# Expert results added into the output in memory, in place of a gather and an add at the end

## The chip, the cores and the metric

The kernel runs on one core of a Trainium2 chip. The metric is the device time of one execution in microseconds (us), taken as the median of three runs. The profile is of one further execution.

## The reference

The input has 4 sequences of 1024 tokens of 128 numbers, 4096 tokens in all. All is float32.

```python
x = x + attention(layernorm(x))        # scores (x*w_lhs)(x*w_rhs)^T, softmax, times layernorm(x)
x = x + experts(layernorm(x))
# experts, N = 4096 tokens, E = 8, hidden 512, TOP_K = 2:
probs = softmax(xf @ router_w.T); topk_probs, topk_idx = top_k(probs, 2)
topk_probs = topk_probs / sum(topk_probs)
h   = gelu(einsum('nc,ech->neh', xf, w_fc) + b_fc)
out = einsum('neh,ehc->nec', h, w_proj) + b_proj
y   = sum over a token's two experts of topk_prob * out
```

So each token has a value x after attention (called `res` here), and two expert results, each times its gate, are added to it.

## The kernel before, in words

Each engine has one instruction stream, written out by hand, and semaphores order them. The kernel has two stages.

**Attention** goes over four batches b (one sequence each, eight groups of 128 tokens). VectorE (DVE) adds the attention to the tokens in SBUF, in `res` (L1302), and raises `res_made` once for each half batch. Then the router picks two experts per token, and GpSimd (POOL) scatters each group of 128 tokens, twice, into the DRAM tensor `slots`, sorted by expert (`dispatch`, L721, 64 scatters). A row of `slots` carries the token's numbers, a row number made from the iota `row_id`, and its gate.

**Experts** go over NTILES = 40 tiles of W = 256 rows of one expert each, with buffers for NB = 8 tiles. The function `run_tiles` gives every engine the same walk: tiles 0 to 15 unrolled, the rest in a loop of eight and an unrolled end. Tiles 0 to 15 use tokens of the first three batches; the sixteen scatters of the last batch are done by POOL in steps 4 to 11 of this walk, two a step, and from tile 16 on SyncE (SP) loads only once all of them have landed (`all_dispatched`, L602 to L605).

For tile k:
- SP loads 256 rows of `slots` into `slots_in` (`load`, L613). From tile 8 on it first waits until DVE has taken the row numbers of an earlier tile.
- TensorE (PE) transposes two tiles ahead (L1146), computes the hidden layer (L1158 to L1160, semaphore `stepped`), and the output projection two tiles behind (L1175). ScalarE (ACT) splits and applies GELU (L911, L919).
- DVE copies gate and row numbers out of `slots_in` (`keep_rows`, L1548, L1549), adds the bias three tiles behind (L1556) and multiplies by the gate (`gate`, L1563, into one of eight buffers `gated`). Both wait on `returned[a]` until the scatters of the tile eight before, which used the same buffer, have landed.
- POOL gives tile k-4 back in step k (`give_back`, L787 to L791): it waits for `stepped`, `row_made` and `gated_made`, and issues two indirect DMAs of 128 rows of 512 bytes (H = 2) to the DRAM tensor `results`. Scatter after scatter goes out; POOL waits for no landing.

`wait_apart` (L505, L506) is a wait followed by a semaphore increment of its own instruction. Rows of a tile that carry no token go to spare rows of `results`, beyond the 8192 that are read.

**The end**: SP waits until all scatters have landed (L618), loads `results` into SBUF in four transfers of 1 MB (L622), DVE adds the two results of each token to `res` (L1592, L1594), and SP stores four parts of 512 KB to the output (L625) and waits for them.

Of the kernel before, what the change touches and what calls it, by code (L numbers as in the profile page):

```python
# [7 lines left out]
P = 128  # L8
F32 = mybir.dt.float32
# [4 lines left out]
ALU = mybir.AluOpType  # L14
# [7 lines left out]
def preln_attention_moe(nc, x, w_lhs, w_rhs, router_wT, w_fc, b_fc, w_proj, b_proj, out):  # L22
# [7 lines left out]
    NT = x.shape[1]  # L30
    D = x.shape[2]
# [3 lines left out]
    B = 4  # L35
    BT = NT // B
    S = BT * P
    N = NT * P
    K = 2
# [5 lines left out]
    H = 2  # L45
    W = H * P
    NB = 8
    NTILES = -(-((K * N + E * (W - 1)) // W) // NB) * NB
# [7 lines left out]


    SPARE = K * N + E * W
    results = nc.dram_tensor("results", [SPARE + NTILES * W, D], F32, kind="Internal").ap()
    assert D == P and NT % (B * 8) == 0 and E == 8  # L60

    with ExitStack() as ctx:  # L62
        def sb(name, shape, dt):
            return ctx.enter_context(nc.sbuf_tensor(name, shape, dt))

        def sem(name):
            return ctx.enter_context(nc.semaphore(name))
# [8 lines left out]
        res = sb("res", [P, NT, D], F32)  # L76
# [40 lines left out]
        raw_fc = sb("raw_fc", [P, E * HID], F32)  # L117
        raw_proj = sb("raw_proj", [P, E * HID], F32)
# [33 lines left out]
        row_id = sb("row_id", [P, NT, K], F32)  # L152
# [40 lines left out]
        gated = [[gated_all[:, a, h, :] for h in range(H)] for a in range(NB)]  # L193
        result_row = [sb(f"result_row{a}", [P, H], I32) for a in range(NB)]
# [49 lines left out]
        res_made = sem("res_made")  # L244
# [40 lines left out]
        gated_made = sem("gated_made")  # L285
        row_made = sem("row_made")
        returned = [sem(f"returned{a}") for a in range(NB)]
        results_in = [sem(f"results_in{b}") for b in range(B)]
        summed = sem("summed")
        added = sem("added")  # L290
        stored = sem("stored")

        block = ctx.enter_context(nc.Block())

# [207 lines left out]
        def wait_apart(eng, sem, value):  # L502


            eng.wait_ge(sem, value)  # L505
            eng.sem_inc(waited_apart, 1)  # L506

        def later(i, least=1):
            return not isinstance(i, int) or i >= least

        def run_tiles(eng, load_experts, step, lag, ahead, between):

            for first in range(0, EARLY, NB):
                load_experts(first)
                for a in range(NB):
                    step(first + a, a)
            between()  # L520
            last = NTILES // NB - ahead
            with eng.Fori(EARLY // NB, last) as i:
                load_experts(i * NB)
                for a in range(NB):
                    step(i * NB + a, a)
            for first in range(last * NB, NTILES, NB):
                load_experts(first)
                for a in range(NB):
                    step(first + a, a)
            load_experts(NTILES)  # L530
            for k in range(NTILES, NTILES + lag):
                step(k, k % NB)
# [37 lines left out]
        def turned_at(k):  # L570

            return k - 1 if not isinstance(k, int) else max(k - 1, 1)
# [6 lines left out]
        @block.sync  # L579
        def _(sp):  # L580
            sp.dma_start(res[:, 0:TU, :], x[:, 0:TU, :]).then_inc(x0_in, 16)
            sp.dma_start(res[:, TU:BT, :], x[:, TU:BT, :]).then_inc(x_in[0], 16)
            sp.dma_start(w_d[:, 0:1], w_lhs).then_inc(w_in, 16)
            sp.dma_start(w_d[:, 1:2], w_rhs).then_inc(w_in, 16)
            sp.dma_start(rwT[:, :], router_wT).then_inc(rw_in, 16)
            for b in range(1, B):
                sp.dma_start(res[:, b * BT:(b + 1) * BT, :], x[:, b * BT:(b + 1) * BT, :]).then_inc(x_in[b], 16)
            sp.dma_start(bfc[:, :, :], b_fc).then_inc(small_in, 16)
            sp.dma_start(bpr[:, :, :], b_proj.unsqueeze(0).to_broadcast([P, E, D])).then_inc(small_in, 16)
            sp.dma_start(raw_fc[:, :], w_fc.rearrange("c e h -> c (e h)")).then_inc(wfc_in, 16)  # L590
            sp.dma_start(raw_proj[:, :], w_proj.rearrange("p e c d -> p (e c d)")).then_inc(wpr_in, 16)

            sp.wait_ge(emptied, 32)
            sp.wait_ge(dispatched[0], 16 * K * 2 * BT)
            sp.wait_ge(dispatched[1], 16 * K * BT)
            sp.wait_ge(w_split, PIECES)
            sp.wait_ge(table_made, 1)

            def all_dispatched():
                for a in range(2):  # L600
                    sp.wait_ge(dispatched[a], 16 * K * 2 * BT)
                sp.wait_ge(table_made, 2)  # L602

            def load(k, a):
                start = sp.value_load(tile_start[0:1, bass.ds(k, 1)], min_val=0, max_val=E * N - W)  # L605

                if later(k, NB):


                    if isinstance(k, int) and k < NB + 3:  # L610
                        sp.wait_ge(stepped, turned_at(k - NB))
                    sp.wait_ge(row_made, k - NB + 2)
                sp.dma_start(xs[a], slots[bass.ds(start, W), :].rearrange("(p h) r -> p h r", h=H)).then_inc(xs_in[a], 16)  # L613
            run_tiles(sp, no_experts, load, 0, 0, all_dispatched)


            for a in range(NB):
                sp.wait_ge(returned[a], 16 * H * NTILES // NB)  # L618
            both = results[0:K * N, :].rearrange("(t p k) d -> p t (k d)", p=P, k=K)
            for b in range(B):  # L620
                half = (raw_fc, raw_proj)[b // 2][:, :].rearrange("p (t x) -> p t x", x=K * D)
                sp.dma_start(half[:, (b % 2) * BT:(b % 2 + 1) * BT, :], both[:, b * BT:(b + 1) * BT, :]).then_inc(results_in[b], 16)  # L622
            for b in range(B):
                sp.wait_ge(added, b + 1)
                sp.dma_start(out[:, b * BT:(b + 1) * BT, :], res[:, b * BT:(b + 1) * BT, :]).then_inc(stored, 16)  # L625
            sp.wait_ge(stored, 16 * B)

        @block.gpsimd
        def _(pool):
            for m in (ident, ident16):  # L630
# [5 lines left out]
                      allow_small_or_imprecise_dtypes=True).then_inc(consts, 1)  # L636
            pool.iota(next_slot[:, :], pattern=[[N, E]], base=0, channel_multiplier=0,
                      allow_small_or_imprecise_dtypes=True).then_inc(consts, 1)
            pool.iota(row_id[:, :, :], pattern=[[K * P, NT], [1, K]], base=0, channel_multiplier=K,
                      allow_small_or_imprecise_dtypes=True).then_inc(consts, 1)  # L640
            for of in (slice(0, EARLY), slice(EARLY, NTILES)):
                pool.iota(tile_id[:, of], pattern=[[1, of.stop - of.start]], base=0, channel_multiplier=0,
# [1 line left out]
            for a in range(NB):  # L644
# [14 lines left out]
                               base=0, pattern=[[1, P]], channel_multiplier=-1).then_inc(consts, 1)  # L659
            for m in (ident, ident16):  # L660
                pool.affine_select(out=m[:, :], in_=m[:, :], compare_op=ALU.not_equal, fill=1.0,
                                   base=0, pattern=[[-1, P]], channel_multiplier=1).then_inc(consts, 1)
# [122 lines left out]
            def give_back(k, a):  # L785

                pool.wait_ge(row_made, k + 1)  # L787
                wait_apart(pool, gated_made, k + 1)
                for h in range(H):
                    pool.indirect_dma_start(out=results[:, :], out_offset=bass.IndirectOffsetOnAxis(ap=result_row[a][:, h:h + 1], axis=0),  # L790
                                            in_=gated[a][h], in_offset=None).then_inc(returned[a], 16)  # L791


            def step(k, a):
                if later(k, 4):

                    pool.wait_ge(stepped, up_at(k) if tile_there(k) else min(k + 1, NTILES + 2))
                    give_back(k - 4, (a - 4) % NB)
                if isinstance(k, int) and 4 <= k < 4 + BT:
                    for i in range(K):  # L800
                        dispatch(B - 1, K * (k - 4) + i)
# [395 lines left out]
        def _(dve):  # L1197
# [386 lines left out]
            run_tiles(dve, expert_loader(dve, expert), step, 3, 0, lambda: dve.wait_ge(table_made, 2))  # L1584


            for b in range(B):
                r = res[:, b * BT:(b + 1) * BT, :]
                half = (raw_fc, raw_proj)[b // 2][:, :].rearrange("p (t k d) -> p t k d", k=K, d=D)
                both = half[:, (b % 2) * BT:(b % 2 + 1) * BT, :, :]  # L1590
                dve.wait_ge(results_in[b], 16)
                dve.tensor_tensor(r, r, both[:, :, 0, :], ALU.add).then_inc(summed, 1)  # L1592
                dve.wait_ge(summed, b + 1)
                dve.tensor_tensor(r, r, both[:, :, 1, :], ALU.add).then_inc(added, 1)  # L1594


# [1 line left out]
_INS = ['L0_attn_x', 'L0_attn_w_lhs', 'L0_attn_w_rhs', 'L0_ffn_router_w', 'L0_ffn_w_fc', 'L0_ffn_b_fc',  # L1598
# [33 lines left out]
```

## Time and profile before

| | us |
|---|---|
| median of 3 runs | 387.96 (387.59 to 389.8) |
| the profiled execution, whole time | 388.4 |
| the profiled execution, span from first to last instruction | 386.6 |

| engine | busy us | share of the span |
|---|---|---|
| PE | 305.1 | 79% |
| PE weight load | 271.2 | 70% |
| DVE | 200.2 | 52% |
| ACT | 199.4 | 52% |
| POOL | 179.7 | 46% |

The page lists busy time by engine; 40 equal slices of the span follow it, then DMA queues, the chain of work that ended last, the costliest groups of instructions, and DMA issues with their time to landing. A name with q (POOLq, SPq) is an engine's sequencer, that is the part which waits and issues. "issue" is time in which an engine waited for nothing that the profile shows.

### The profile page before, as it was taken

The page shows a single profiled execution, that of the slowest core. Times are in us where ns is not written, and L with a number is a line of the kernel's source. Part 1 is how long each engine was busy: PE and PEld are TensorE (multiplying, and loading weights), DVE is VectorE, ACT ScalarE, POOL GpSimd, SP SyncE. Part 2 cuts the span into 40 slices and gives each one's busy share as a digit, 9 for nine tenths or more (in the row PEclk, how much of TensorE's full clock was granted, in tenths as well). Part 3 has the DMA queues.
Part 4 walks back from the last instruction along what each step waited for, and adds up shares of the span by engine and source line. Part 5 has one row for each costly group of instructions (what it writes and reads, how often), then busy time and mean ns, then how long its engine had stood idle before and what let it go on. Part 6 is the DMA issues. An engine that isn't in the chain of part 4 may idle for free. (4 is left out here: it accounts for less than half of the span.)

```text
span 386.6 us, 8174 instructions
## 1 busy us (share of the span) xinstructions
PE 305.1 (79%) x2292; PEld 271.2 (70%) x2293; DVE 200.2 (52%) x755; ACT 199.4 (52%) x409; POOL 179.7 (46%) x236
## 2 busy tenths in 40 slices
PE   2689999998999899999128999806999999999000
PEld 1468788776978789878116999805999999998000
DVE  4656488696757566788624563301333233333136
ACT  4206438696047733472319777702677677774000
POOL 7200034181846244547730277774455555555600
PEclk9989998999899999999857999975999999999655
DMA  7910000003100000001122232114222222111189
GB/s 225 428 55 2 0 3 0 3 0 110 36 21 30 28 29 28 30 28 50 42 76 70 56 94 71 50 55 121 73 85 84 77 80 68 58 42 42 48 298 353
DMA packets 17155, 29.47 MB, mean 76 GB/s; under 512 B 3808, under 2 KB 13024, under 8 KB 16864
## 3 DMA queue, kind: packets, MB, share of 16 engines
q1 hardware_dynamic: 12224, 18.46, 14.5%
q0 software_dynamic: 4896, 10.58, 8.4%
q8 instruction: 18, 0.29, 0.3%
q14 instruction: 17, 0.14, 0.1%
HBM read 16.36 MB, written 12.66 MB: 75 GB/s over the span
## 5 line engine op out<-in xcount | busy, mean ns | idle before, releaser
L790 POOL DMA_INDIRECT results<-prob,result_row x80 | 77.0, 962 | 71.9 <-PE sc_ps L1160 51.8
L721 POOL DMA_INDIRECT slots<-stage,slot x64 | 62.4, 975 | 52.7 <-ACT prob L832 29.8
L1175 PE MATMUL av_ps<-raw_proj,raw_fc 128*128 x640 | 79.1, 278 | 1.0 <-DVE h_all L1556 1.0
L919 ACT ACTIVATE raw_fc<-sc_ps,bfc,scale_down 128x256 f32<-128x256 f32 x160 | 77.3, 572 | 2.1 <-PE sc_ps L1160 2.1
L1175 PEld LDWEIGHTS av_ps<-raw_proj,raw_fc 128*128 128x128 f32 x640 | 75.6, 194 | 1.9 <-issue 1.3
L983 PEld LDWEIGHTS av_ps<-h_all,prob 128*128 128x128 f32 x512 | 66.9, 191 | 4.4 <-DVE res L1302 1.0
L983 PE MATMUL av_ps<-h_all,prob 128*128 128x137 f32 x512 | 69.4, 283 | 0.0
L1556 DVE TENSOR_TENSOR h_all<-av_ps,bpr 128x256 f32<-128x256 f32 x40 | 17.0, 424 | 81.1 <-PE sc_ps L1160 76.4
L911 ACT ACTIVATE h_all<-bank 128x512 f16<-128x512 f16 x40 | 23.9, 598 | 60.9 <-PE sc_ps L1160 48.4
L1158 PE MATMUL sc_ps<-h_all,wfc_hi 128*128 128x256 f16 x160 | 45.3, 283 | 1.8 <-ACT h_all L911 1.8
L1160 PE MATMUL sc_ps<-h_all,wfc_lo 128*128 128x256 f16 x160 | 45.2, 283 | 0.0
L1159 PE MATMUL sc_ps<-h_all,wfc_hi 128*128 128x256 f16 x160 | 45.2, 283 | 0.0
L1146 PE MATMUL bank<-ident,slots_in 128*128 128x128 f16 x160 | 16.5, 230 | 29.7 <-DMA slots_in<-slots 29.6
L1146 PEld LDWEIGHTS bank<-ident,slots_in 128*128 128x128 f16 x160 | 12.5, 103 | 31.3 <-DMA slots_in<-slots 15.7
L1279 DVE TENSOR_REDUCE neg_piece<-bank 128x1 f32<-128x512 f32 x32 | 22.1, 689 | 19.9 <-PE bank L964 11.6
L844 ACT ACTIVATE h<-res,shift,rstd 128x128 f32<-128x128 f32 x32 | 15.5, 485 | 27.3 <-POOL shift L690 27.3
L962 PE MATMUL bank<-hT_hi,q_hi 128*128 128x512 f32 x48 | 23.8, 496 | 5.7 <-ACT prob L832 5.7
L832 ACT ACTIVATE prob<-sc_ps 128x512 f32<-128x512 f32 x32 | 19.1, 598 | 14.9 <-PE sc_ps L975 9.3
L832 ACT ACTIVATE prob<-bank 128x512 f32<-128x512 f32 x32 | 19.0, 595 | 11.7 <-PE bank L975 9.7
L1279 DVE TENSOR_REDUCE neg_piece<-sc_ps 128x1 f32<-128x512 f32 x32 | 21.8, 685 | 3.5 <-PE sc_ps L964 3.4
L1563 DVE TENSOR_SCALAR prob<-h_all,row_gate 128x128 f32<-128x128 f32 x80 | 20.2, 297 | 3.3 <-DVE h_all L1556 2.2
L963 PE MATMUL bank<-hT_lo,q_hi 128*128 128x512 f32 x48 | 20.3, 422 | 0.0
(174 smaller groups left out, 509.6 us busy)
## 6 DMA issues: line engine op xcount, KB each, us to landing
slots_in<-slots SPq DMA_DIRECT2D x40, 130.0 KB, 2.1
raw_fc<-in_w_fc_dram SPq DMA_DIRECT2D x1, 2048.0 KB, 11.1
raw_proj<-in_w_proj_dram SPq DMA_DIRECT2D x1, 2048.0 KB, 15.5
raw_fc<-results SPq DMA_DIRECT2D x2, 1024.0 KB, 6.5
raw_proj<-results SPq DMA_DIRECT2D x2, 1024.0 KB, 10.5
out_dram<-res SPq DMA_DIRECT2D x4, 512.0 KB, 4.8
res<-in_x_dram SPq DMA_DIRECT2D x3, 512.0 KB, 5.7
results<-prob,result_row POOLq DMA_INDIRECT x80, 2.2
```

Source lines behind the costliest of these rows:

```text
L721: pool.indirect_dma_start(out=slots[:, :], out_offset=bass.IndirectOffsetOnAxis(ap=slot[:, n, k:k + 1], axis=0), in_=stage[:, b % 2, t, k, ...
L790: pool.indirect_dma_start(out=results[:, :], out_offset=bass.IndirectOffsetOnAxis(ap=result_row[a][:, h:h + 1], axis=0), in_=gated[a][h], ...
L832: act.activation(probT[:, m % RING, :], exp_bank(n), ACT.Exp).then_inc(exp_made, 1)
L911: act.activation(xT[:, a % NH, :], bank[a % 2][:, :].bitcast(F16)[:, 0:2 * W], ACT.Copy).then_inc(xT_made, 1)
L919: ins = act.activation(hid[:, a % NH, c, :], up_ps(a, c), ACT.Gelu_apprx_tanh, bias=bfc[:, e, c:c + 1], scale=scale_down[:, 0:1])
L983: mm = pe.matmul(att[:, t, 0:AUG], probT[:, m % RING, t * P:(t + 1) * P], h_aug[:, b % 2, exp_rows(n), :], start=(n % BT == 0 and t % 2 == ...
L1146: mm = pe.transpose(o[:, part * W + h * P:part * W + (h + 1) * P], x, ident16[:, :])
L1158: pe.matmul(o, wfc_hi[:, e, w], xT[:, a % NH, 0:W], start=True, stop=False, skip_group_check=True)
L1159: pe.matmul(o, wfc_hi[:, e, w], xT[:, a % NH, W:2 * W], start=False, stop=False, skip_group_check=True)
L1160: mm = pe.matmul(o, wfc_lo[:, e, w], xT[:, a % NH, 0:W], start=False, stop=True, skip_group_check=True)
L1175: mm = pe.matmul(o, hid[:, a % NH, c, s], wpr[:, e, c, :], start=(c == 0 and h == 0), stop=(c == HC - 1), skip_group_check=True)
L1279: dve.tensor_reduce(neg_piece[:, r // TU, r % TU, c:c + 1], block_bank(n), AX_X, ALU.max, negate=True).then_inc(max_made, 1)
```

## The change

Each part of the attention result is stored to the output tensor as soon as it is made (`lay_out`): three parts before SP's waits of the expert stage, the fourth just before the load of tile 8. The row number in `row_id` is now the token's row in the output, the same for both of its experts. `give_back` scatters into the output with an add in the DMA (`compute_op`), and drops rows whose number is beyond the last token (`bounds_check`). Before the first tile it waits for the four stores; before every later tile it waits until both scatters of the tile before have landed. The tensor `results`, its reading back, the DVE additions and the stores at the end are gone.

```diff
-    results = nc.dram_tensor("results", [SPARE + NTILES * W, D], F32, kind="Internal").ap()
+    out_rows = out.rearrange("p t d -> (p t) d")
...
+            def lay_out(b):
+                sp.wait_ge(res_made, 2 * b + 2)
+                sp.dma_start(out[:, b * BT:(b + 1) * BT, :], res[:, b * BT:(b + 1) * BT, :]).then_inc(out_laid, 16)
+            for b in range(B - 1):
+                lay_out(b)
             sp.wait_ge(emptied, 32)
...
             def load(k, a):
+                if isinstance(k, int) and k == NB:
+                    lay_out(B - 1)
...
             for a in range(NB):
                 sp.wait_ge(returned[a], 16 * H * NTILES // NB)
-            both = results[0:K * N, :].rearrange("(t p k) d -> p t (k d)", p=P, k=K)
-            for b in range(B):
-                half = (raw_fc, raw_proj)[b // 2][:, :].rearrange("p (t x) -> p t x", x=K * D)
-                sp.dma_start(half[:, (b % 2) * BT:(b % 2 + 1) * BT, :], both[:, b * BT:(b + 1) * BT, :]).then_inc(results_in[b], 16)
-            for b in range(B):
-                sp.wait_ge(added, b + 1)
-                sp.dma_start(out[:, b * BT:(b + 1) * BT, :], res[:, b * BT:(b + 1) * BT, :]).then_inc(stored, 16)
-            sp.wait_ge(stored, 16 * B)
...
-            pool.iota(row_id[:, :, :], pattern=[[K * P, NT], [1, K]], base=0, channel_multiplier=K,
+            pool.iota(row_id[:, :, :], pattern=[[1, NT], [0, K]], base=0, channel_multiplier=NT,
...
                 pool.wait_ge(row_made, k + 1)
                 wait_apart(pool, gated_made, k + 1)
+                if isinstance(k, int) and k == 0:
+                    pool.wait_ge(out_laid, 16 * B)
+                if later(k):
+                    wait_apart(pool, returned[(a - 1) % NB], 16 * H * (k // NB + (1 if a else 0)))
                 for h in range(H):
-                    pool.indirect_dma_start(out=results[:, :], ...
-                                            in_=gated[a][h], in_offset=None).then_inc(returned[a], 16)
+                    pool.indirect_dma_start(out=out_rows, ...
+                                            in_=gated[a][h], in_offset=None, bounds_check=N - 1, oob_is_err=False,
+                                            compute_op=ALU.add).then_inc(returned[a], 16)
...
-            for b in range(B):
-                r = res[:, b * BT:(b + 1) * BT, :]
-                half = (raw_fc, raw_proj)[b // 2][:, :].rearrange("p (t k d) -> p t k d", k=K, d=D)
-                both = half[:, (b % 2) * BT:(b % 2 + 1) * BT, :, :]
-                dve.wait_ge(results_in[b], 16)
-                dve.tensor_tensor(r, r, both[:, :, 0, :], ALU.add).then_inc(summed, 1)
-                dve.wait_ge(summed, b + 1)
-                dve.tensor_tensor(r, r, both[:, :, 1, :], ALU.add).then_inc(added, 1)
```

## Rows read from the trace of the kernel before

**Rows 1.** Chain that ended last, from 355 us: start, length, what.
```profile
355.07 0.04 POOLq L506
355.11 0.74 issue
355.85 0.51 POOL results L790
...
358.12 0.74 issue
...
365.18 2.22 DMA results<-prob,result_row
...
369.83 11.25 DMA raw_proj<-results
```
**Rows 2.** Timeline of the end, all engines: start, length, engine, line, what.
```profile
375.36 8.59 SPq L625 DMA_DIRECT2D out_dram<-res  x4
```
**Rows 3.** Stretches: length; busy us of PE, PEld, DVE, ACT, POOL; PE clock, DMA.
```profile
219.00:260.00 41.00, 31.11 (x299) 29.71 (x298) 15.59 (x71) 23.70 (x50) 30.97 (x33) 0.94 0.23 68
264.00:351.00 87.00, 86.80 (x806) 82.00 (x807) 27.90 (x125) 60.18 (x124) 48.29 (x51) 0.97 0.26 75
367.40:386.60 19.20, 0.00 (x0) 0.00 (x0) 9.79 (x8) 0.00 (x0) 0.00 (x0) 0.50 0.90 328
```
**Rows 4.** Timeline of POOL while it also scatters the last batch.
```profile
219.29 1.07 POOL L790 DMA_INDIRECT results<-prob,result_row  x1 [22.26 <-PE sc_ps L1160]
...
256.10 0.96 POOL L790 DMA_INDIRECT results<-prob,result_row  x1 [0.30 <-issue]
...
258.63 0.96 POOL L721 DMA_INDIRECT slots<-stage,slot  x1 [0.30 <-issue]
259.89 0.95 POOL L790 DMA_INDIRECT results<-prob,result_row  x1 [0.30 <-issue]
261.15 0.96 POOL L790 DMA_INDIRECT results<-prob,result_row  x1 [0.30 <-issue]
```
**Rows 5.** The same timeline after it; the last two rows are tile 39.
```profile
268.05 0.96 POOL L790 DMA_INDIRECT results<-prob,result_row  x1 [3.40 <-PE sc_ps L1160]
...
332.88 0.96 POOL L790 DMA_INDIRECT results<-prob,result_row  x1 [1.09 <-PE sc_ps L1160]
...
336.20 0.96 POOL L790 DMA_INDIRECT results<-prob,result_row  x1 [1.09 <-PE sc_ps L1160]
...
363.92 0.96 POOL L790 DMA_INDIRECT results<-prob,result_row  x1 [0.30 <-issue]
365.18 0.96 POOL L790 DMA_INDIRECT results<-prob,result_row  x1 [0.30 <-issue]
```
**Rows 6.** Chain that ended last, at the last batch's final scatter.
```profile
258.63 2.27 DMA slots<-stage,slot
...
264.06 0.61 PE bank L1146 x4
```
**Rows 7.** One line or tile: duration ns min/median/max; landing of its DMAs (L790, then slots_in).
```profile
L790 POOL DMA_INDIRECT results<-prob,result_row x80: 953/960/1067, 219.3 to 365.2; - x80
...
DMA to landing us min/median/max: 2.2/2.2/2.8
...
DMA to landing us min/median/max: 2.0/2.1/3.9
```
**Rows 8.** Duration of the two direct DMAs that POOL issues.
```profile
L711 POOL DMA_DIRECT2D slots<-raw_fc x2: 762/916/1071, 86.4 to 87.5; - x2
```
**Rows 9.** DMA queue of POOL, 364.0 to 367.4 us: packets, MB, share of 16 engines.
```profile
q0 software_dynamic: 96, 0.20, 17.9%
```
**Rows 10.** Timelines of DVE and SP where the last part of res and the early loads are.
```profile
189.34 1.13 DVE L1302 SCALAR_TENSOR_TENSOR res<-av_ps,inv_sum,res 128x128 f32<-128x128 f32 x4
...
197.86 7.98 SPq L613 DMA_DIRECT2D slots_in<-slots  x8
```
**Rows 11.** Output stores of the end: landing.
```profile
DMA to landing us min/median/max: 2.6/4.8/7.0
```

More of the change, by code:

```diff
@@ L287, in preln_attention_moe @@
         returned = [sem(f"returned{a}") for a in range(NB)]
[L288 to L291, printed above, removed]
+        out_laid = sem("out_laid")
         block = ctx.enter_context(nc.Block())
@@ L788, in give_back @@
                 wait_apart(pool, gated_made, k + 1)
+                if isinstance(k, int) and k == 0:
+                    pool.wait_ge(out_laid, 16 * B)
+                if later(k):
+                    wait_apart(pool, returned[(a - 1) % NB], 16 * H * (k // NB + (1 if a else 0)))
                 for h in range(H):
-                    pool.indirect_dma_start(out=results[:, :], out_offset=bass.IndirectOffsetOnAxis(ap=result_row[a][:, h:h + 1], axis=0),
-                                            in_=gated[a][h], in_offset=None).then_inc(returned[a], 16)
+                    pool.indirect_dma_start(out=out_rows, out_offset=bass.IndirectOffsetOnAxis(ap=result_row[a][:, h:h + 1], axis=0),
+                                            in_=gated[a][h], in_offset=None, bounds_check=N - 1, oob_is_err=False,
+                                            compute_op=ALU.add).then_inc(returned[a], 16)
             def step(k, a):
```

## The prediction
> **What bounds the kernel now.** I read the chain of waits that ended last first, backwards from the end. Its last stretch has no matrix work at all. The last scatter of tile 39 is issued at 365.18 us and lands 2.22 us later, at 367.40 [rows 1]. From there to the end of the span, 386.6, are 19.2 us: the four transfers of `results` back (the chain holds 11.25 us of one of them), the DVE additions, and the four stores. In that stretch PE and POOL are busy for 0.00 us and the DMA engines for 0.90 of the time [rows 2, 3]. The change removes this stretch whole, so it is its gross gain.
>
> Then I read who sets the pace before it. Between 264 and 351 us PE is busy for 86.8 of 87 us [rows 3], and POOL's first scatters of consecutive tiles stand 3.32 us apart, each after an idle time that PE ends (332.88 to 336.20) [rows 5]. So PE is the bound there, and POOL has room: a pair of scatters takes 1.27 us from the first start to the second and 0.96 us for the second, 2.23 of 3.32 us. Before 264 us it is the other way: from 219.29 to 259.89 POOL issues back to back, four indirect DMAs a tile [rows 4], and PE waits for the last of them, issued at 258.63 and landed 2.27 us later; PE goes on at 264.06 [rows 6].
>
> The slack of POOL in the long stretch, 3.32 less 2.23, is 1.1 us a tile. The change puts into it a wait for a landing.
>
> **The early stores.** The last part of `res` is made by 190.5 us. The eighth load of SP is issued by 205.84 us, and the fourth store follows it at once; SP waited before its first load (197.86) anyway for scatters [rows 10]. A store of this size lands after 2.6 to 7.0 us [rows 11], so by 213 us, and the first scatter into the output stands at 219.29 [rows 4]. That leaves 6 us of cover. Loads 8 and on queue behind 512 KB in the same DMA engines; at the 328 GB/s of [rows 3] that is 1.6 us once, and the pace there is POOL's, so I cost it at nothing (1.6 us if that cover were gone). The other three stores are issued while SP waits and the attention stage hardly uses the DMA. Taking the iota with other steps costs nothing.
>
> **The wait for the tile before.** Behind this wait on POOL stand the two scatters of the tile, in steps 4 to 11 the two `slots` scatters of the last batch, and every later tile. The cost has three terms, from the start of a tile's first scatter to that of the next:
> - 1.27 us from the first to the second scatter (363.92 to 365.18) [rows 5];
> - L, from the start of the second scatter to its landing;
> - G, from the landing to the start of the next scatter. With POOL's queue empty, the increment of `wait_apart` takes 0.04 us and the scatter starts 0.74 us after it, in both places of the chain where it can be seen (355.11 and 358.12) [rows 1]. With 0.02 us to see the semaphore, G is 0.80. The 0.30 us of back-to-back scatters [rows 4] hide this start, because the sequencer hands the next DMA over while the one before is being written; a wait for the landing takes that away, since the landing comes 1.26 us after POOL has finished. So 0.30 is the lower bound of G and 0.80 the value I take.
>
> For L the trace has a plain scatter: 2.2 us in the median, up to 2.8 [rows 7]. An adding one also reads 64 KB of the destination. The lower bound is no extra, 2.22. The upper bound is a whole read before the write: a load from DRAM lands in 2.1 us [rows 7], together 4.3. The data of one scatter keep a DMA engine busy for only 17.9% of 3.4 us, over three scatters, 0.20 us [rows 9]; one more read of as many bytes is nearer to a doubling of this than to a second transfer with its own start and landing. I take 0.43 us more, about twice that busy time, L = 2.65, near the lower end.
>
> The Trainium skill (Collectives: The Full Stack, "The bandwidth ceiling: the fold count and why AG ≠ RS ≠ AR") says that an add in the DMA is slower for its two source reads, not for the arithmetic. By this rule only the 0.20 us of moving is added, L = 2.42, and the time would be some 7 us below my forecast; no row here shows an add.
>
> The issue of a scatter on POOL, 0.96 us, I keep. Two direct DMAs of POOL with many more rows take 0.76 to 1.07 us [rows 8], so more descriptors need not cost more. Upper bound: 0.3 us more for each adding scatter, with dropped rows and the add; below the present price is nothing to gain, as the same rows are walked.
>
> While POOL also scatters the last batch, the wait is hidden. The next tile's first scatter stands 3.79 us behind the second of the tile before (256.10 to 259.89) [rows 4], and L + G is 3.45. With L over 2.99 it would show, seven times, and it would delay PE's restart at 264.06 by as much.
>
> From tile 8, at 259.89, the period is P = 1.27 + 2.65 + 0.80 = 4.72 us in place of PE's 3.32. Tiles 8 to 39 are 31 periods: 146.3 us, so tile 39 starts at 406.2. The routing of the reference's inputs fills 35 tiles of the 40, so tiles 35 to 39 drop all rows and read nothing: I give back 0.43 us in the four periods that follow one of them, 1.7 us, which puts the start at 404.5. The last landing is then 1.27 + 2.22 later, 408.0, and 0.3 us end the program. That is a span of 408.3 against 386.6. The profiled execution took 388.4, 1.8 us more than its span, so I forecast 410.1 us for one like it. The median of the runs, 387.96, lies 0.4 us below that execution; I say 410.
>
> What the removal gives, 19.2 us, and what the wait takes, 40.9 us (367.40 to 408.0 and 0.3), make the 21.7 us of the difference. PE, DVE and SP don't add to it: DVE waits at tile k only for the scatters of tile k-8, four tiles behind the one that POOL is giving back, so the engines run ahead until the buffers are full and then go at POOL's pace. A PE that idles in each tile may get the lower clock (it stands at 0.97 now and at 0.81 or less only when idle), which doesn't matter while its 3.32 us have 1.4 us of room.
>
> **Rivals.**
> 1. *The landing is seen quickly.* If the next scatter starts 0.30 us after a landing that is no later than now, P is 1.27 + 2.22 + 0.30 = 3.79 us. PE then still sets the start of tile 10 (268.05), tile 39 starts 29 periods later at 378.0, lands at 381.4, and the run takes 383.5 us, 1.2% faster. The mechanism turns at P = 3.94: there 29 periods and 3.8 us more reach 386.6. For it speak the 0.30 us gaps; against it that each is between DMAs already queued, and that both idle starts have 0.74. At the extreme, P below 3.32, the whole 19 us would be gained, 369.5 us. 7%, of which 2% is for a P so near the turning point that no change can be told.
> 2. *No dearer landing, slow start.* L = 2.22, G = 0.80, P = 4.29: tile 39 at 392.9, landed at 396.4, 398.5 us. This is the lower part of my mechanism; 25% for a time of 393 to 403.
> 3. *A dear add.* L = 3.2: P = 5.27, 31 periods, 3.9 us back for the empty tiles, 1.5 us from the early steps, 426.5 us. If instead each adding scatter is issued 0.3 us slower, the period grows by 0.6, and the eight tiles before by 16 x 0.3: 18.6 and 4.8 us over my forecast, 433 us. With the full upper bound, L = 4.3, P is 6.37, the early steps pay 7 x 1.3 us, and the run takes 464 us. 25% for over 418 us.
> 4. *The output is not what the early stores left in time*, so that tile 0 waits on `out_laid`. It decides from 6 us of delay on, and then every microsecond shows. 2%, inside the above.
>
> **Chances and range.** My mechanism with L of 2.3 to 3.0 has 43%, rival 2's stretch 25%, rival 3 25%, rival 1 7%. The range, 394 to 436 us, leaves out rival 1, the lowest edge, and a landing dearer than 3.4 us. Faster than 0.5% below, 0.05; within 0.5% (what a measurement of this kernel can tell from no change), 0.02; slower, 0.93.
>
> **What would show it.** In the trace after, the stretch behind the last landing is gone, within 1 us. POOL's pairs stand 4.3 to 5.3 us apart from tile 8 on, with an idle time that ends on a DMA landing in place of PE, and the chain that ended last is a row of POOL and DMA pieces from 259 us on with hardly any PE. PE's 86.8 of 87 us falls to some 70%. The landing of L790 reads 2.6 to 2.7 and its issue 0.96. Before 259 us nothing moves. The last five tiles are a little quicker. I am wrong if the pairs keep 3.3 us, if the landing reads over 3.4, if the issue grows, or if the time from landing to start is 0.3.

## The result, and the profile after

The changed kernel takes 469.66 us in the median of four runs (466.92 to 471.05), the kernel before 388.3 on the same chip: 1.206 times as long, 95% interval 1.200 to 1.212. I forecast 410 with 394 to 436 as the range. The direction was right, the size was not: 81 us more in place of 22.

The first lines of the page after, by engine and in 40 slices:
```profile
span 467.5 us, 8305 instructions
PE 321.5 (69%) x2292; PEld 281.2 (60%) x2293; DVE 193.0 (41%) x747; ACT 199.2 (43%) x409; POOL 227.7 (49%) x236
PE   2889999899989988069994039976676767563000
POOL 6200343554717447601688864455555555545553
```
POOL is busy for 227.7 us against 179.7, with as many instructions. PE drops from 9 to between 5 and 7 tenths from 304 us on (slice 27), and POOL works into the last slice: the stretch of reading back, in which POOL had nothing to do, is gone.

POOL's scatters, answering to [rows 7]: the line's duration in ns (min/median/max) and the landing in us.
```profile
L794 POOL DMA_INDIRECT out_dram<-prob,result_row x80: 1540/1551/1682, 219.4 to 460.6; - x80
...
DMA to landing us min/median/max: 2.7/3.3/5.1
```
The issue took 1.55 us, not 0.96. The landing is counted from the start of the issue, so 0.59 of its 1.1 us more are the issue again; what follows the issue went from 1.26 to 1.75.

Three stretches of POOL's timeline, answering to [rows 4, 5]: tile 8; two tiles of the steady stretch (29, with both its scatters, and 30); three of the tiles 35 to 39, which the prediction counts as all dropped (36, 37 and 39).
```profile
272.37 1.60 POOL L794 DMA_INDIRECT out_dram<-prob,result_row  x1 [0.31 <-issue]
...
399.83 1.55 POOL L794 DMA_INDIRECT out_dram<-prob,result_row  x1 [2.54 <-DMA out_dram<-prob,result_row]
401.68 1.55 POOL L794 DMA_INDIRECT out_dram<-prob,result_row  x1 [0.30 <-issue]
405.89 1.55 POOL L794 DMA_INDIRECT out_dram<-prob,result_row  x1 [2.66 <-DMA out_dram<-prob,result_row]
...
441.53 1.55 POOL L794 DMA_INDIRECT out_dram<-prob,result_row  x1 [2.01 <-DMA out_dram<-prob,result_row]
...
446.98 1.55 POOL L794 DMA_INDIRECT out_dram<-prob,result_row  x1 [2.04 <-DMA out_dram<-prob,result_row]
...
458.70 1.55 POOL L794 DMA_INDIRECT out_dram<-prob,result_row  x1 [2.32 <-issue]
460.56 1.55 POOL L794 DMA_INDIRECT out_dram<-prob,result_row  x1 [0.30 <-issue]
```
In the brackets the releaser of a tile's first scatter is now a landing (for 29 of the 39 tiles that wait), where before it was PE: the engine that sets the pace is POOL with its DMA. The period is 6.06 us here and 6.01 in the mean from tile 8 to tile 39 (272.37 to 458.70, 31 periods), against 3.32 before. Empty tiles cost 5.4 to 6.0 us, not much less.

The chain that ended last, one period of it (start, length, what):
```profile
425.95 3.35 DMA out_dram<-prob,result_row
429.34 0.06 issue
429.41 0.03 POOLq L794
429.44 0.49 issue
429.93 0.03 POOLq L794
429.96 0.20 issue
430.15 0.33 POOL out_dram L794
```
From the landing (429.30) to the next scatter (430.15) are 0.85 us, and from there to the second scatter, 432.00, 1.85. With 3.3 for the landing this is the whole 6.0; PE isn't in it.

The end, in one row each of the changed kernel and, second, of the kernel before: DRAIN, the last long instruction in POOL's sequencer, with its duration in ns and its start.
```profile
L63 POOLq DRAIN  x1: 8234/8234/8234, 459.0 to 459.0; - x1
```
```profile
L62 POOLq DRAIN  x1: 12537/12537/12537, 361.5 to 361.5; - x1
```
After the change the last landing is at 463.3 and the span ends at 467.5, with the DRAIN at 467.2. Before, it ended at 374.1, under the reading back; it was hidden there.

**Where the 80.9 us of span are** (467.5 less 386.6):

| part | before | after | difference |
|---|---|---|---|
| start of tile 8's first scatter | 259.89 | 272.37 | +12.5 |
| from there to tile 39's first scatter | 104.0 | 186.3 | +82.3 |
| from there to the last landing | 3.5 | 4.6 | +1.1 |
| from the last landing to the end | 19.2 | 4.2 | -15.0 |

### The profile page after: what moved, and what is told of

It is laid out like the page before. It is cut to its first block, busy times and chain, and to the rows that moved or that the text cites. A ratio compares the mean times of both kernels' runs of the same rounds, so it can differ in the third digit from the quotient of the medians.

```text
span 467.5 us, 8305 instructions
## 1 busy us (share of the span) xinstructions
PE 321.5 (69%) x2292; PEld 281.2 (60%) x2293; DVE 193.0 (41%) x747; ACT 199.2 (43%) x409; POOL 227.7 (49%) x236
## 3 DMA queue, kind: packets, MB, share of 16 engines
HBM read 12.16 MB, written 12.66 MB: 53 GB/s over the span
## 4 chain that ended last, share of the span: by engine, by line
PE 33%; issue 21%; DMA 21%; POOL 9%; ACT 7%; DVE 5%; POOLq 2%; SPq 1%; ACTq 0%; DVEq 0%
DMA out_dram<-prob,result_row 18%; PE av_ps L988 7%; PE av_ps L1180 6%; POOL out_dram L794 4%; POOL slots L720 4%; PE bank L967 2%; PE sc_ps L1163 2%; PE sc_ps L1165 2%; PE sc_ps L1164 2%; ACT prob L837 2%; PE bank L969 2%; PE bank L968 2%; DVE neg_piece L1284 2%; PE sc_ps L967 1%; ACT stage L851 1%
## 5 line engine op out<-in xcount | busy, mean ns | idle before, releaser
L794 POOL DMA_INDIRECT out_dram<-prob,result_row x80 | 125.0, 1562 | 119.5 <-DMA out_dram<-prob,result_row 74.3
L1180 PE MATMUL av_ps<-raw_proj,raw_fc 128*128 x640 | 91.0, 302 | 44.6 <-DVE h_all L1561 36.9
L1180 PEld LDWEIGHTS av_ps<-raw_proj,raw_fc 128*128 128x128 f32 x640 | 84.6, 213 | 51.3 <-issue 51.0
L1553 DVE COPY row_gate<-slots_in 128x2 f32<-128x2 f32 x40 | 6.7, 167 | 120.7 <-DMA out_dram<-prob,result_row 91.4
L1163 PE MATMUL sc_ps<-h_all,wfc_hi 128*128 128x256 f16 x160 | 45.9, 287 | 1.7 <-ACT raw_fc L924 1.7
L1164 PE MATMUL sc_ps<-h_all,wfc_hi 128*128 128x256 f16 x160 | 45.8, 286 | 0.0
L967 PE MATMUL bank<-hT_hi,q_hi 128*128 128x512 f32 x48 | 23.8, 495 | 5.7 <-ACT prob L837 5.7
```

Source lines behind the costliest of these rows:

```text
L794: pool.indirect_dma_start(out=out_rows, out_offset=bass.IndirectOffsetOnAxis(ap=result_row[a][:, h:h + 1], axis=0), in_=gated[a][h], in_of ...
L967: pe.matmul(o, q_hi[:, a, rows], hT_hi[:, a, cols], start=True, stop=False, skip_group_check=True)
L1163: pe.matmul(o, wfc_hi[:, e, w], xT[:, a % NH, 0:W], start=True, stop=False, skip_group_check=True)
L1164: pe.matmul(o, wfc_hi[:, e, w], xT[:, a % NH, W:2 * W], start=False, stop=False, skip_group_check=True)
L1180: mm = pe.matmul(o, hid[:, a % NH, c, s], wpr[:, e, c, :], start=(c == 0 and h == 0), stop=(c == HC - 1), skip_group_check=True)
```

## The experiments

The changed kernel does three things to a scatter at once: an add, a bound (rows beyond the last token are dropped), a wait. The first four kernels take them apart. They ran on one chip, where the kernel before took 388.59 us. Where the results are never read, the output holds the attention part alone.

### e1: nothing read back, plain scatters
```diff
 (from the changed kernel)
-    wait_apart(pool, returned[(a - 1) % NB], ...)
-    out=out_rows, ... bounds_check=N - 1, oob_is_err=False, compute_op=ALU.add
+    out=results[:, :], ...          # a row of its own for each result, never read
```


> The changed kernel without its wait, its add and its drop of rows: plain scatters into a DRAM tensor with a row of its own for each result, as before; the results are never read, so the output holds the attention part alone. It prices what the change removes. If the stretch behind the last landing is worth its whole 19.2 us and the early stores are hidden: 369 to 370 us. If the early stores or the order of SP's loads cost something: more than 372 us. POOL's pairs stay 3.3 us apart, issue 0.96, landing 2.2.

Measured: 375.59 us (374.13 to 377.69), 0.965 of before, interval 0.959 to 0.971. Issue 0.96, landing 2.2, and the last scatters stand where they stood. The end of POOL's timeline, and its DRAIN:
```profile
365.32 0.96 POOL L792 DMA_INDIRECT results<-prob,result_row  x1 [0.30 <-issue]
```
```profile
L63 POOLq DRAIN  x1: 12530/12530/12530, 361.7 to 361.7; - x1
```
The last result lands at 367.54, the span ends at 374.4: removing the reading back gives 12.2 us of span, not 19.2. Of the other 7.0, 6.7 us are POOL's DRAIN, which lasts until 374.2 and had lain under the end. The run is over the 372 us that I had set as the sign of dear early stores, but they aren't the cause: the first scatter stands at 220.3 against 219.3, and the last at 365.3 against 365.2.

### e2: the add alone
```diff
 (from e1)
+    compute_op=ALU.add
```


> As the kernel without a tail, with the add in the DMA and still no bound and no wait (same rows of its own, never read). Theory A, the add alone makes the scatter dear: issue 1.55 us on POOL, landing 3.3 us, POOL becomes the bound without any wait (two issues of 1.85 us a tile, 3.7 against PE's 3.32; 16 x 0.59 us more before tile 8), about 391 us. Theory B, the bound and the dropped rows make the issue dear: issue 0.96, landing perhaps longer, 369 to 371 us.

Measured: 399.4 us (397.44 to 401.36), 1.028 of before (1.022 to 1.034). Theory A holds: issue and landing are those of the changed kernel, without a bound or a wait. Two rows of POOL's timeline:
```profile
352.96 1.55 POOL L792 DMA_INDIRECT results<-prob,result_row  x1 [0.30 <-issue]
354.81 1.55 POOL L792 DMA_INDIRECT results<-prob,result_row  x1 [0.30 <-issue]
```
1.85 us a scatter, 3.71 a tile: POOL is over PE's 3.32 by its issues alone. The add makes 23.8 us over e1, and with it the kernel is slower than before even if no tile waits for another. The time is 8 us above the 391 expected; in the profiled execution (397.4) the DRAIN again ends it, at 395.4, 3.9 us after the last landing.

### e3: the bound alone
```diff
 (from e1)
+    bounds_check=K * N - 1, oob_is_err=False
```


> As the kernel without a tail, plain scatters, but rows without a token are dropped by the bound; no add, no wait. Theory A (the add): issue 0.96, 369 to 371 us. Theory B (the bound): issue 1.55, about 391 us, and the landing stays 2.2.

Measured: 379.66 us (377.57 to 380.03), 0.974 of before (0.969 to 0.979), so 4 us over e1. Issue and landing against e1:
```profile
L792 POOL DMA_INDIRECT results<-prob,result_row x80: 977/980/1075, 221.6 to 368.6; - x80
...
DMA to landing us min/median/max: 2.1/2.3/3.4
```
Theory B falls. The bound brings 0.02 us more an issue and a register move in POOL's sequencer for each scatter, and dropping the rows that carry no token gains nothing that shows. Where the whole 4 us lie wasn't taken apart.

### e4: the wait alone
```diff
 (from the kernel before; read back as before)
+    if later(k):
+        wait_apart(pool, returned[(a - 1) % NB], 16 * H * (k // NB + (1 if a else 0)))
```


> The kernel before with one change: POOL waits for both scatters of the tile before. Plain scatters, results read back as before. It prices the wait by itself. By the sum of the prediction (1.27 + 2.22 + 0.80 = 4.29 us a tile from tile 8 on, start at 259.9): last landing at 396.4, 417 us. If a landing is seen at once (0.30): 3.79 us a tile, 402 us. If something beyond this chain is lost, more than 422 us.

Measured: 423.39 us (422.57 to 425.32), 1.090 of before (1.084 to 1.095). POOL's timeline, late:
```profile
381.03 0.96 POOL L792 DMA_INDIRECT results<-prob,result_row  x1 [2.04 <-DMA results<-prob,result_row]
382.29 0.96 POOL L792 DMA_INDIRECT results<-prob,result_row  x1 [0.30 <-issue]
385.29 0.96 POOL L792 DMA_INDIRECT results<-prob,result_row  x1 [2.04 <-DMA results<-prob,result_row]
```
The usual period is 4.26 to 4.28 us, of 1.26, 2.22 and 0.78: the prediction's 1.27, 2.22 and 0.80. The start of tile 8 (259.41) didn't move. The time is over the 422 us that I had set as the sign of something beyond this chain. The 6 us over my sum come from eight of the 31 periods, of 4.46 to 6.32 us; behind six of them stands a landing of 2.5 to 4.3 us, four of these at tiles 9 to 14. What made those landings long I didn't test.

### e5: add and bound, no wait
```diff
 (from e1)
+    bounds_check=K * N - 1, oob_is_err=False, compute_op=ALU.add
```


> The changed kernel with its add and its bound, but rows of its own for each result in a DRAM tensor that is never read, and therefore no wait for the tile before (the output holds the attention part alone). Theory A, cost of the add on POOL plus cost of the wait, which only together stand in a row: without the wait POOL goes at two issues a tile, 3.7 us, about 403 us (the add-only kernel's 399 and the bound's 4). Rival: the adds themselves slow memory down beyond the landing (many adds in flight): clearly over 410 us.

Measured on a second chip (before 387.93): 397.5 us (395.57 to 400.63), 1.022 of before (1.019 to 1.026). The rival, slow memory under many adds, falls. The bound's 4 us don't show here, where POOL is bound by its issues (e2 stood at 1.028 of its own before, with overlapping intervals). Against the changed kernel, which differs by the wait and the shared rows, the wait is worth 72 us here and 35 in e4. That it is the wait and not the shared rows, the landing says: 3.3 us in the median in both. The period explains the two prices: 3.32 to 4.27 with plain scatters, 3.71 to 6.01 with adding ones.

### e6 and e7: what the issue of an adding scatter is paid by
```diff
 (e6, from e2)                       (e7, from e2)
+    result_row[a][0:P // 2, ...]    +    in_=gated[a][h][:, 0:D // 2]
+    in_=gated[a][h][0:P // 2, :]         (and results has rows of D // 2)
```


> The add-only kernel, each scatter with 64 rows in place of 128 (half of the results left out). If the 0.59 us that the add puts on the issue is paid row by row: issue 1.26 us or less. If it is paid once per instruction: near 1.55 us. The landing behind the issue (1.75 us) shrinks by at most 0.2.

> The add-only kernel, 128 rows of 256 bytes in place of 512 (half of each result left out). If the issue is paid by rows: 1.55 us as before. If by bytes: near 1.26 us.

One execution of each, 387.22 and 399.86 us, on the second chip. The two lines, e6 and e7 in this order:
```profile
L792 POOL DMA_INDIRECT results<-prob,result_row x80: 1406/1417/1583, 216.8 to 375.9; - x80
```
```profile
L792 POOL DMA_INDIRECT results<-prob,result_row x80: 1542/1552/1683, 220.6 to 390.8; - x80
```
Half the rows take 0.13 us off the issue, half the bytes nothing. By these two points 64 rows cost 0.13 us and an instruction of no rows would cost some 1.28 (an extrapolation). So most of the 1.55 us is paid per instruction. Neither expected figure, 1.26 and 1.55, is met. Of the 0.59 us that the add puts on the issue, rows can make at most twice 0.13, 0.27; how much less isn't shown, since no plain scatter of 64 rows was run. At least 0.32 are paid once per instruction.

### e10: a direct DMA with an add
```diff
 (from e2)
-    pool.indirect_dma_start(out=results[:, :], out_offset=..., in_=gated[a][h], in_offset=None, compute_op=ALU.add)
+    pool.dma_start(results[(a * H + h) * P:(a * H + h + 1) * P, :], gated[a][h], accum_op=ALU.add)
```


> The add-only kernel with direct adding DMAs of the same 64 KB in place of the indirect ones (to fixed rows; the results are in the wrong place and never read). If the add makes an issue on POOL dear whatever the addressing: near 1.5 us. If only the indirect form is dear: under 1.1 us, as the direct DMAs without an add (0.76 to 1.07). The landing behind the issue tells the same for the memory side: 1.75 us if the second read makes it.

```profile
L792 POOL DMA_DIRECT2D results<-prob x80: 859/1108/1930, 229.7 to 370.1; - x80
...
DMA to landing us min/median/max: 2.5/3.0/3.7
```
One execution, 379.73 us, on the third chip (below). The issue takes 1.11 us in the median, at my upper figure, and two back to back take 1.76: the direct form is far from 1.55. The long issue belongs to the indirect DMA with an add. What follows the issue is 3.0 less 1.11, about 1.9 us, against 1.75 in the adding scatter and 1.26 in the plain one, so that part goes with the add and not with the indirect form. A direct DMA of this size without an add wasn't run.

### e9: a wait for the tile two before
```diff
 (from e5)
+    if later(k, 2):
+        wait_apart(pool, returned[(a - 2) % NB], 16 * H * (k // NB + (1 if a > 1 else 0)))
```


> The changed kernel with rows of its own for each result (never read; the output holds the attention part alone), with add and bound, and with a wait for the tile two before in place of the tile before. If the wait is dear only because POOL stands empty from issue to landing, the scatters of the tile between cover it (5.6 us from a tile's second scatter to the first of the tile after next, against 3.3 + 0.85): POOL stays at 3.7 us a tile, 397 to 400 us. If a wait on a landing costs by itself (its start of 0.85 us each time): 3.7 + 0.55, about 415 us.

This kernel, e10, e11 and e12 ran on a third chip, where the kernel before took 412.02 us (409.86 to 413.73), so their times stand only beside that. Measured: 406.89 us (403.77 to 407.33), 0.988 of before there (0.984 to 0.992). The 397 to 400 expected were for the other chips, and the 0.988 can't be set beside e5's 1.022: on this chip the plain scatters of e11 stand 3.61 us a tile apart from tile 10 to tile 35, where the kernel before, with PE setting the pace, has 3.37 in the trace that the document started from. A kernel at POOL's own pace loses less there. POOL's timeline decides, and it is the add-only kernel's to the hundredth:
```profile
350.44 1.55 POOL L794 DMA_INDIRECT results<-prob,result_row  x1 [0.30 <-DMA results<-prob,result_row]
352.30 1.55 POOL L794 DMA_INDIRECT results<-prob,result_row  x1 [0.30 <-issue]
354.15 1.55 POOL L794 DMA_INDIRECT results<-prob,result_row  x1 [0.30 <-issue]
```
3.71 us a tile: a wait for a landing costs nothing when another tile's scatters lie between. The changed kernel can't have it as it stands: two neighbouring tiles of different experts can hold the same token, and nothing would keep their two additions to its row apart, so this form was tried only with rows of its own. Nor would a better placed wait have been enough on the first two chips: e2 and e5 have no wait at all and take 1.028 and 1.022 of before.

### e11: the last four tiles' scatters left out
```diff
 (from e1, plain scatters; the results of tiles 36 to 39 are left out, and SP's last waits count one tile less for these buffers)
-    give_back(k - 4, (a - 4) % NB)
+    if not isinstance(k, int) or k < NTILES:
+        give_back(k - 4, (a - 4) % NB)
```


> The kernel without a tail (plain scatters) with the scatters of tiles 36 to 39 left out; POOL waits for the same steps. It asks what the 6.7 us between the last landing and the end are. If POOL's last instruction (DRAIN) ends 7.9 us after the last indirect DMA that POOL issued: POOL is free at some 362 us and the span ends there. If it takes 7.9 us from the moment it is reached: 366 us. If it is tied to the program's end otherwise: 374 us as before.

390.57 us, one execution on the third chip, so I read the distances. The last scatter is issued at 377.06, and:
```profile
L63 POOLq DRAIN  x1: 7257/7257/7257, 381.3 to 381.3; - x1
```
POOL had been idle for 3.3 us when it came to the DRAIN, and it still took 7.26. In e1 and in the kernel before it ended 7.9 us after the last issue's end. So it takes some 7.3 to 7.9 us from when it is reached and POOL has nothing more to issue; of my three cases the second is the nearest, and being done earlier doesn't save it. In the adding kernels it is shorter, 5.1 to 5.7 us after the last issue. What POOL does in it stays open.

### e8 and e12: the reading back made cheaper
If what the change wanted to remove is 4 MB read back, halve it. e8 keeps the kernel before and scatters and reads the gated results as float16 (each result is rounded once); e12 also sums the two halves in float16 before they meet the float32 tokens.
```diff
 (e8, from the kernel before)
-    results = nc.dram_tensor("results", [...], F32, kind="Internal").ap()
+    results = nc.dram_tensor("results", [...], F16, kind="Internal").ap()
     (gated and the buffers read into are float16 views of the same memory)
 (e12, from e8)
-    dve.tensor_tensor(r, r, both[:, :, 0, :], ALU.add)
+    dve.tensor_tensor(both[:, :, 0, :], both[:, :, 0, :], both[:, :, 1, :], ALU.add)
 ...
-    dve.tensor_tensor(r, r, both[:, :, 1, :], ALU.add)
+    dve.tensor_tensor(r, r, both[:, :, 0, :], ALU.add)
```


> The kernel before with the gated results scattered and read back as float16 (256-byte rows): 2 MB read back in place of 4. If the end is bound by bytes of the read back (4 MB over some 11 us), its stretch shrinks by 4 to 5 us: about 383.5 us. If by the number of rows (256-byte pieces move no faster than 512-byte ones): 387 to 389 us. The output differs by the rounding of the two results to float16.

> The kernel with float16 results read back, where DVE was busy without a gap over eight additions of 1.23 us; here the first addition of each pair adds the two float16 halves to each other and the second adds their float16 sum to the float32 tokens. If an addition of float16 alone is quicker (0.6 us): 4 x 0.6 us less, about 383 us. If it costs the same 1.23 us: 385 us.

e8: 385.29 us (384.19 to 388.77) against 387.93, 0.992 of before (0.990 to 0.995). The end in the stretches view:
```profile
370.50:386.90 16.40, 0.00 (x0) 0.00 (x0) 9.54 (x8) 0.00 (x0) 0.00 (x0) 0.50 0.74 256
```
It is 16.4 us where it was 19.2 in [rows 3], and the DMA share fell from 0.90 to 0.74 while DVE adds without a gap: the transfers had filled the stretch, and after 2.8 us of gain, in place of the 4 to 5 expected, DVE is the bound: it starts 3.8 us into the stretch and works at its eight additions until 384.0. e12 answers with DVE's additions, at the end of its timeline:
```profile
391.00 0.69 DVE L1592 TENSOR_TENSOR raw_fc<-raw_fc 128x1024 f16<-128x1024 f16 x1 [11.29 <-DMA raw_fc<-results]
391.73 1.22 DVE L1594 TENSOR_TENSOR res<-res,raw_fc 128x1024 f32<-128x1024 f32 x1
```
An addition of float16 alone takes 0.69 in place of 1.22 us, and the stretch is 14.7 us long. On its chip e12 took 405.95 us (403.35 to 408.51) against 412.02, 0.986 of before (0.982 to 0.991). Both beat the kernel before, by less than 2%, and the changed one; the two weren't timed on one chip, so the gap between them isn't measured.

## Why the prediction was wrong

**The failed step.** "The issue of a scatter on POOL, 0.96 us, I keep." It took 1.55 (e2, and 0.98 for the bound in e3). The row I leaned on was of direct DMAs without an add, and it says nothing of an indirect one with it; e10 shows that the form decides (1.11 against 1.55). That "the issue grows" stood among my signs of being wrong, and it did. The bound of 0.3 us that I gave for it was a guess too small by half, and with it the range. The term counts twice in a period, as the first issue and inside L: 1.17 us of 31 periods are 36 us, and 10.2 us of the 12.5 before tile 8.

Point by point, of the 59.2 us between my span (408.3) and the measured one:

- *The 31 periods*: 186.3 us against 144.6, 41.7 more. 36 of them are the issue. The rest is G, 0.85 in place of 0.80 (a register move for the bound lies in it), the part of L below, and five periods of 6.18 to 6.76 us.
- *Before tile 8*: I said nothing moves. It moved by 12.5: sixteen issues of 1.6 us there in place of 0.96 are 10.2, and the landings of tiles 0 and 1, 5.1 and 3.9 us, left 1.8 us of idle time. The rest of the wait was hidden there, as I said; e4 shows no delay at all in this stretch.
- *The part of L behind the issue*: 1.75 us against my 1.69. The size was right partly by luck: I took "about twice" a busy time of 0.20, and knew nothing of the packets. That it comes with the time that the DMA engines are busy is borne out. POOL's DMA queue in a stretch of 15 us, first after, then before (packets, MB, share of 16 engines):
```profile
q0 software_dynamic: 576, 0.23, 18.3%
```
```profile
q0 software_dynamic: 288, 0.59, 12.1%
```
  The first is four scatters of 144 packets, 0.69 us of each engine per scatter; the second nine of 32 packets, 0.20 us. The 0.49 us more are the 0.49 that the landing grew behind the issue. The same queue in steady stretches of e2 (44.56 us), e6 (40) and e7 (45):
```profile
q0 software_dynamic: 3456, 1.57, 39.5%
```
```profile
q0 software_dynamic: 1843, 0.76, 27.9%
```
```profile
q0 software_dynamic: 3561, 0.81, 33.1%
```
  Per scatter these are 0.73, 0.48 and 0.60 us of each engine, and behind the issue the landing takes 1.75, 1.6 and 1.65 (landings of 3.3, 3.0 and 3.2 in the median): less the 0.20 and 1.26 of a plain scatter, 0.53, 0.28 and 0.40 beside 0.49, 0.3 and 0.4. Half the rows (80 packets) help more than half the bytes (144 still). The Trainium skill (Collectives: The Full Stack, "The bandwidth ceiling: the fold count and why AG ≠ RS ≠ AR") puts the price of a reduction's add on two source reads in place of one; by that rule 0.20 becomes 0.40. The trace has 0.69 with 4.5 times as many packets, so the rule gives 0.20 of the 0.49 more. The second read itself shows in no count: the profile has 12.16 MB read from memory in e1 and in e2 alike.
- *G*: 0.78 in e4, 0.85 after, against 0.80. The reading of the two idle starts [rows 1] against the gaps of 0.30 [rows 4] held, and with it the rejection of rival 1.
- *The wait by itself*: 4.27 us a tile in e4 against 4.29.
- *The empty tiles* (35 and on): visible, 2.7 us to land in place of 3.3. The four periods that follow one took 5.41, 5.45, 6.00 and 5.72 us, together 1.5 us less than four usual ones, where I had 1.7; in the last two POOL's start took longer, for a reason that stays open.
- *The end*: the last tile took 4.6 us from its first scatter to its last landing against 3.5, 1.1 more. Behind that landing I set 0.3 us; it is 4.2, because POOL's DRAIN had been hidden. That is 3.9 us of the miss, and the gain of removing the tail is 12.2 us with plain scatters (e1), not 19.2.
- *The early stores*: hidden, as predicted.
- Rival 3 (a dear add) was the right case by name, but its price went with a bound that no row supported.
- Two slips of the working changed nothing here: the period at which rival 1 turns is 3.96 us and not 3.94 (268.05 and 29 periods and 3.8 make 386.6), and the slack of POOL under PE's 3.32 us is 0.8 us and not 1.1, since the pair was counted as 2.23 without the 0.30 behind its second scatter (tiles 8 and 9 of the kernel before stand 2.53 apart: 259.89 and 262.42).

The sum of effects measured alone misleads as well: over e1, the add (23.8 us) and the bound (4) and, over the kernel before, the wait (34.8) and the removed end (-13.0) make some 50 us; together they make 81. Per tile of the steady stretch it can be read: over POOL's own 2.53 us the add makes 1.18 more (3.71) and the wait 1.74 (4.27), but of each the slack of 0.8 under PE's 3.32 is hidden while it comes alone. Together it is hidden once, and the longer landing, 0.49, which costs nothing unless something waits for it, comes on top: 5.94 of the 6.01.

## What to carry to other kernels

An adding scatter removes bytes at the end, but in this kernel its price sat on the issuing engine, for the greater part per instruction, in every tile: multiply it by the number of instructions before counting what it saves. POOL's wait for its own last DMA turned landing and start-up into a serial chain, issue + landing + 0.8 us here; with one independent batch between issue and wait it was free. Where a row of the profile shows a neighbour of the new operation and not the operation itself, the bound on its cost must come from how different the neighbours are (here an add, a second source and another form of descriptor), not from a small margin on the nearest.

## What the runs showed of the hardware that I had not expected

- An indirect DMA on POOL takes 0.96 us to issue, with an add 1.55; 64 rows in place of 128 make it 1.42, 256 bytes a row in place of 512 change nothing (1.55). A direct DMA with an add took 1.11.
- An adding scatter of 128 rows moved in 144 packets in place of 32, and kept each DMA engine busy for 0.69 us in place of 0.20; of 64 rows, in 80 packets, for 0.48.
- POOL's DRAIN at the end of the program took 7.3 to 7.9 us after plain scatters, even when POOL had been idle for 3.3 us, and 5.1 to 5.7 after adding ones.
- Three chips gave 388.6, 387.9 and 412.0 us for the same kernel.
